# A decoder kernel whose first phase issues each whole-array product as two halves of 64 output partitions

## The reference

```
x = x + L0_attn(layernorm(x))       # mixes x with its shifted copy: dd, then r, k, v, g, w = lerp(...) @ W.T;
                                    # a scan over time for each of 16 heads; group norm; (out * g) @ out_w.T
x = x + L0_xattn(layernorm(x), ctx) # q = x @ wq + b; k, v = ctx @ wk, wv + b, 16 heads of 64, plus 128 memory
                                    # keys and values; softmax(q k / 8) v; @ wo + b
x = x + L0_ffn(layernorm(x))        # router_logits = x @ router_w.T, best 2 of 8 experts
x = x + L1_attn(...); x = x + L1_xattn(...); x = x + L1_ffn(...)
```

## Time and profile before

| | us |
|---|---|
| median of 3 runs | 1446.36 |
| lowest, highest | 1444.64, 1446.71 |
| profiled execution | 1450.02 |
| its span, first to last instruction | 1448.1 |
| TensorE busy in the span | 1312.5 (91%) |
| TensorE weight loads | 964.8 (67%) |
| VectorE busy | 1092.4 (75%) |
| ScalarE busy | 1090.3 (75%) |
| GpSimd busy | 636.4 (44%) |

### The profile page before, as it was taken

How to read it: one execution, slowest core, us unless ns; L and a number is a source line. 1 busy time by engine, 2 the same in 40 slices (tenths; PEclk the granted TensorE clock), 3 DMA queues, 4 the chain that set the end, 5 groups by cost and what they waited for, 6 DMA issues and landing times.

```text
span 1448.1 us, 42973 instructions
## 1 busy us (share of the span) xinstructions
PE 1312.5 (91%) x15457; PEld 964.8 (67%) x15457; DVE 1092.4 (75%) x2601; ACT 1090.3 (75%) x2903; POOL 636.4 (44%) x839
## 2 busy tenths in 40 slices
PE   4259999999999999999984999989989999999996
PEld 1125666666666666667673999967667777777764
DVE  6998889999899988877665344566768788686676
ACT  2128999999999999999992666657677777877763
POOL 0011423353444424320205545357775776655664
PEclk9999999999999999999996999989999999999997
DMA  6942242423224232011013332230101010000000
GB/s 141 245 119 64 52 103 53 101 62 81 60 60 107 56 95 61 16 65 33 24 31 95 91 92 82 58 134 19 31 11 40 10 41 10 24 24 2 25 9 16
DMA packets 82333, 88.49 MB, mean 61 GB/s; under 512 B 15568, under 2 KB 71504, under 8 KB 77520
## 3 DMA queue, kind: packets, MB, share of 16 engines
q1 hardware_dynamic: 77456, 77.10, 20.5%
q0 software_dynamic: 4096, 8.40, 2.0%
q10 hardware_dynamic: 576, 0.26, 0.1%
HBM read 64.76 MB, written 17.83 MB: 57 GB/s over the span
## 4 chain that ended last, share of the span: by engine, by line
PE 64%; DVE 16%; ACT 10%; issue 6%; POOL 2%; DMA 2%; another core or an unknown queue 0%; ACTq 0%; DVEq 0%; SPq 0%; POOLq 0%
PE P L832 7%; PE P L994 7%; PE P L2175 7%; PE P L1615 4%; PE P L1648 4%; PE P L850 3%; PE P L976 3%; ACT pr L1055 3%; PE P L953 3%; PE P L964 3%; PE P L948 3%; PE P L2246 3%; PE P L2193 3%; PE P L2123 2%; PE P L871 2%
## 5 line engine op out<-in xcount | busy, mean ns | idle before, releaser
L1055 ACT ACTIVATE pr<-P,nm 128x256 f32<-128x256 f32 x512 | 239.1, 501 | 6.0 <-DVE nm L1253 5.9
L1253 DVE TENSOR_REDUCE nm<-P 128x4 f32<-128x1024 f32 x128 | 156.2, 1220 | 25.5 <-PE P L832 23.3
L2415 ACT ACTIVATE et<-P 128x1024 f32<-128x1024 f32 x128 | 131.1, 1025 | 42.4 <-PE P L2182 41.4
L832 PE MATMUL P<-kt_w,qt 64*128 64x256 f32 x1024 | 145.2, 402 | 4.6 <-ACT pr L1055 4.6
L1037 ACT COPY ptS<-P 128x512 f32<-128x512 f32 x256 | 138.2, 599 | 8.7 <-PE P L850 8.2
L1028 ACT ACTIVATE pr<-pr,ri 128x256 f32<-128x256 f32 x254 | 119.5, 536 | 24.1 <-DVE pr L1226 23.5
L740 POOL TENSOR_TENSOR kv_qk<-kv_qk,mixing 128x512 f32<-128x512 f32 x48 | 61.1, 1272 | 152.1 <-DVE pr L1226 152.1
L1711 ACT ACTIVATE hT<-P,mixing 128x128 f32<-128x128 f32 x284 | 81.4, 368 | 61.4 <-PE P L1615 54.1
L734 POOL TENSOR_TENSOR kv_qk<-kv_qk,r_w 128x512 f32<-128x512 f32 x48 | 61.0, 1271 | 145.0 <-DVE pr L1226 99.4
L1055 ACT ACTIVATION_READ_ACCUMULATOR pr<-P,nm 128x1 f32 x512 | 118.6, 232 | 0.0
L2553 DVE TENSOR_REDUCE qS<-P 128x8 f32<-128x1024 f32 x64 | 78.3, 1224 | 45.5 <-PE P L2175 45.1
(11 more groups left out here) (373 smaller groups left out, 3828.2 us busy)
## 6 DMA issues: line engine op xcount, KB each, us to landing
kv_qk<-scr_v SPq DMA_DIRECT2D x16, 1024.0 KB, 8.1
r_w<-scr_r SPq DMA_DIRECT2D x16, 1024.0 KB, 10.7
xt<-scr_xs SPq DMA_DIRECT2D x71, 64.0 KB
scr_ys<-yt SPq DMA_DIRECT2D x71, 64.0 KB, 1.5
x<-in_x SPq DMA_DIRECT2D x8, 256.0 KB, 10.2
scr_v<-mixing SPq DMA_DIRECT2D x8, 256.0 KB, 2.5
scr_r<-mixing SPq DMA_DIRECT2D x8, 256.0 KB, 2.0
xb<-in_x SPq DMA_DIRECT2D x8, 256.0 KB, 3.5
```

Of the source, the lines that this page charges most:

```text
L832: m = nc.tensor.matmul(scores(s)[:, hh, cc * KEYS:(cc + 1) * KEYS], QT[part, c, b * T:(b + 1) * T], keys, start=True, stop=True)
L1055: e = nc.scalar.activation(pr[:, s % 3, h * KEYS:(h + 1) * KEYS], scores(s)[:, h // 2, (h % 2) * KEYS:(h % 2 + 1) * KEYS], ACT.Exp, bias=n ...
L1253: nc.vector.tensor_reduce(nm[:, s % 3, 0:4].rearrange("p (a h) -> p a h", a=2), scores(s).rearrange("p a (h k) -> p a h k", k=KEYS), AX.X, ...
L2415: nc.scalar.activation(et[:, u % 4, :, :, :], turned_scores(u), ACT.Exp).then_inc(S["h_exp"], 1)
```

## The change

A helper `product` stands in the first phase's `tensor_program`. It issues one product as two: output partitions 0 to 63 with the weight columns 0 to 63, then 64 to 127 with the columns 64 to 127, both with the same moving operand and the same start and stop flags. The semaphore is raised by the second half. All products of the first phase that used the whole array go through it: dd, r, v, k, w, g, o, out, lg, cum, keys, queries, values, the output projection and the last sums. Not changed are the scores, the weighted sums, and all transposes, those of the whole array among them. No wait and no other engine's program is changed. The second and third phases stay.

```diff
+                def product(out, weights, moving, start=True, stop=True):
+                    for c in range(0, 128, HALF):
+                        m = nc.tensor.matmul(out[c:c + HALF], weights[:, c:c + HALF], moving, start=start, stop=stop)
+                    return m
...
-                        nc.tensor.matmul(bank7, wA[:, 0, :], XS[:, :, 0:T], start=True, stop=True)\
-                          .then_inc(S["b7"], 1)
+                        product(bank7, wA[:, 0, :], XS[:, :, 0:T]).then_inc(S["b7"], 1)
...
-                            m = nc.tensor.matmul(bank7[:, b * T:(b + 1) * T], KV[:, 7, b * T:(b + 1) * T], centre[:, :],
-                                                 start=True, stop=True)
+                            m = product(bank7[:, b * T:(b + 1) * T], KV[:, 7, b * T:(b + 1) * T], centre[:, :])
...
-                            nc.tensor.matmul(P[:, 3, :], wk[:, c * 128:(c + 1) * 128], ctP[:, g % 2, :],
-                                             start=True, stop=True).then_inc(S["b_kp"], 1)
+                            product(P[:, 3, :], wk[:, c * 128:(c + 1) * 128], ctP[:, g % 2, :]).then_inc(S["b_kp"], 1)
...
-                        nc.tensor.matmul(P[:, 4, :], ctP[:, g % 2, b * T:(b + 1) * T],
-                                         wv[:, half * 512:(half + 1) * 512], start=True, stop=True)\
+                        product(P[:, 4, :], ctP[:, g % 2, b * T:(b + 1) * T], wv[:, half * 512:(half + 1) * 512])\
                           .then_inc(S["b_vp"], 1)
...
-                            m = nc.tensor.matmul(P[:, 4, 0:128], aoT[:, b, 4 * half + c, :], wo[:, 4 * half + c, :],
-                                                 start=(c == 0), stop=(c == 3))
+                            m = product(P[:, 4, 0:128], aoT[:, b, 4 * half + c, :], wo[:, 4 * half + c, :],
+                                        start=(c == 0), stop=(c == 3))
```

## The result

The changed kernel takes 1436.01 us (median of 6 runs, 1434.17 to 1436.72) against 1446.53 us for the kernel before (median of 6). The ratio is 0.9928 with a 95% interval from 0.9916 to 0.9940, so 10.5 us less. The forecast was 1433 with a range of 1425 to 1442.

A forecast was written before the change was run, and what follows sets the result against it. TensorE was taken to set the pace, with ScalarE a few per cent behind. Savings of 10.8 + 1.6 + 0.6 + 0.4 = 13.4 us gave 1436.6 from the profiled execution, 1433 us from the median; range 1425 to 1442.

The forecast's parts named there:

- The price of a change of tiling: Packed attention steps: 0.09 us drain and 0.05 and 0.05 us of weight load saved, 5.39 to 5.19 us.
- The two packed steps with whole-array transposes: Steps with L807 or L912: the tiling change only moves, 0.14 us more and 0.14 less, so nothing in sum.
- A pair of halves costs what a whole instruction costs: All split products: halves run side by side, 0.86 us per 512-column product, nothing gained or lost.
- halves in line: Rival: second half starts 0.43 us late at 512 columns, 1447 to 1488 us; chance 0.09 together with any other loss.
- The small bf16 sums: One step of each group: eight whole sums of 0.21 us become sixteen halves of 0.4, 0.2 us more.
- What reaches the end in the middle groups: Nine of sixteen steps keep 0.20 us, 1.8 us a group, 10.8 us for six groups.
- What the transposes wait for: Transposes on TensorE wait 1.1 us in a step where VectorE's normalisation holds ScalarE; steps leading up lose their saving.
- The sign that I had set for the waits: Packed steps at 5.19 us with longer waits between them and a middle group above 83.5 us.
- the waits swallow more: Rival: ScalarE and VectorE hand the saving back as idle time, half lost, 1440 us (1438 to 1443.5); chance 0.20.
- The last two groups: ScalarE is next, idle 0.12 us in a light step; gains of 1.6 us and 0.6 us.
- Before step 0: Half loads save 0.1 us at the lower clock's pace for about four products in the chain: 0.4 us.

The follow-up runs named there:

- the two partial kernels: Against the kernel before: halves only for values, output projection and last sums, 1444.06 us; halves for all products but those, 1454.87 us.
- e_scalar_after: Changed kernel with ScalarE normalising only 64 of each head's 256 probabilities: 1429.40 us, ratio 0.9884 to the kernel before.
- e_both_after: Changed kernel with VectorE's step-7 scan put behind the next normalisation and GpSimd's bias addition held back: 1437.29 us, ratio 0.9946 to the kernel before.
- e_pool_after: Changed kernel with VectorE's running sum moved to GpSimd from the third group on: 1447.22 us, ratio 0.9985 to the kernel before.

## Why the prediction held, point by point

**The price of a change of tiling: right.** 0.20 us for a packed step was forecast, 0.22 measured (5.39 to 5.17), and the two partial kernels show the same price with the other sign: 5.54 with one change more, 5.36 to 5.39 with the same number. The two packed steps with whole-array transposes (3 and 9 of a group) stay at 4.89, as forecast.

**A pair of halves costs what a whole instruction costs: right**, at 128 and at 512 columns. The rival of halves in line is out: it asked for a second half 0.43 us late, and no product shows that. The Trainium skill's rule behind it (TensorE: Matmul & The Clock Gate, Part 3, matmuls start strictly in program order) doesn't describe the two passes of one half and the first pass of the other here: the code issues the whole product of the first half ahead of the second's, and in the trace one matmul of each starts within 10 ns (443.603 and 443.610 us), the next two 0.43 us later, four in 0.86 us in all.

**The small bf16 sums: the term was too large.** 0.2 us more was forecast, 0.06 measured. Within 0.2 to 0.4 us, but at its lower part. The Trainium skill (TensorEngine Tiling (Array Packing), Restrictions: no fast weight load with column tiling) leads one to expect a loss here; the loss is there and small, 0.27 us against 0.21. That it comes from this rule no run here shows.

**The router's logits: a term that I left out.** With 8 columns a product is all weight load. Whole loads follow one another at 0.11 us, pairs of half loads at 0.06: 0.42 us less in step 11. That step saves 0.63 us in six of the eight groups (1 to 6), 0.43 more than another packed step, so 2.6 us in all were in no term of mine. I had read that a pair of halves costs as much as a whole from products of 128 columns, where the streaming takes as long as the load.

**What reaches the end in the middle groups: the term was too large**, and this is the step that made the forecast 3 us too low. I took nine steps at 0.20 us, 10.8 us for six groups; the profiles have 6.1. And 2.1 of these 6.1 are the logits'. In the steps of groups 1 to 4, steps 0, 1, 4 and 13 save 0.2 each, 12 and 15 do in the fifth group alone, and step 11 saves 0.63. But in the last three of these groups step 5 lasts 0.32 to 0.37 us longer than before (5.13 to 5.45 in the fifth) and step 10 0.10 to 0.27; in the second to fourth group step 12 lasts 0.2 longer; steps 7 and 8 stay as they were. I had counted steps that wait for VectorE today as lost, and had not looked at steps that would start to wait. The waits of the fifth group answer to the earlier trace rows:

```profile
PEld P L789 <- ACT ptS L1035: 6.9, 15, 1.3
...
PEld P L856 <- issue: 3.8, 6, 1.4
...
ACT pr L1026 <- DVE pr L1224: 3.3, 4, 1.8
```

For the transposes TensorE's loads wait 3.8 us where it was 2.2, and ScalarE waits for VectorE's normalisation as before, 3.3 us. The first row has the values and the output projection together, since the helper's line is one; before, they were two rows (L976 3.5 us in 7 waits, L964 2.1 in 6), so 6.9 us in 15 waits stand against 5.6 in 13.

What the transposes wait for is not what I had read. I had put their wait down to VectorE's normalisation. But the unit that a step transposes was normalised 5 to 6 us earlier. The code also makes them wait until VectorE has read PSUM bank 4, which they write: the values with their bias (L1205, `V<-P,bv`) or the sum into the residual (L1212, `xb<-xb,P`) of the step before. Steps 5 and 8 of the fifth group, VectorE and TensorE:

```profile
467.41 0.29 DVE L1212 TENSOR_TENSOR xb<-xb,P 128x128 f32<-128x128 f32 x1
467.95 0.71 PE L856 MATMUL P<-ident,pr 64*128 64x64 f32 x16 [0.35 <-DVE xb L1212]
...
482.50 1.21 DVE L1192 TENSOR_TENSOR_SCAN kv_qk<-mixing,kv_qk 128x512 f32<-128x512 f32 x1
483.63 0.66 DVE L1205 TENSOR_TENSOR V<-P,bv 128x512 f32<-128x512 f32 x1
484.50 0.71 PE L856 MATMUL P<-ident,pr 64*128 64x64 f32 x16 [1.02 <-issue]
```

The transposes start 0.25 us after the addition ends in the one and 0.21 in the other, and the same distance, 0.21 to 0.31, stands in every step of this group in which they start late: 2, 5, 8 and 10 before the change; 2, 5, 7, 8, 10 and 14 after it. In step 5 the addition ends 1.22 us into the step, where it was 0.76 before: TensorE's steps 0, 1 and 4 are 0.2 us shorter each, and VectorE, whose instructions follow one another without a gap here, is not faster. That is how savings came to be eaten.

The experiments fit as far as they go: moving work of VectorE or GpSimd shortens the long step and lengthens the next ones, and leaves the sum. That taking VectorE's work away widens the distance is likely but not sure, and an order of VectorE's queue with the bank read ahead of the scan and the norms was not tried on its own.

The sign that I had set for the waits, a group above 83.5 us with packed steps at 5.19, came in two of the four middle groups (83.7 and 83.5). So the rival "the waits swallow more" was right for these groups, where more than half of the forecast 1.8 us was lost; over the whole kernel other terms made up for it.

**The last two groups: right in kind.** ScalarE bounds them, as forecast from the earlier trace rows, and `e_scalar_after` shows it. I took 2.2 us; the profiles say 3 to 5. The logits' step is 0.63 us of the rest. The others I set too low because I took ScalarE's idle time for the bound of each single step: several light steps of the last group but one now take 4.31 us, less than the 4.43 to 4.46 that ScalarE needs in a row of them, and ScalarE catches up in the heavier steps between.

**Before step 0:** 0.4 us was forecast, with a clock at the lower level that I had taken from the pace of one product alone; the windows of the profile list 1.00 for that stretch, so the level is not shown. The profiles show the steps start 2.2 us earlier, the run with halves only there shows no gain above 1.2. Open.

The sum came out near in part by luck: two terms that were too small (the last groups, the logits) stood against one that was too large. Without the 2.6 us of the logits, which I had not seen, the gain would have been some 8 us where 13.4 were forecast.

## What to carry to other kernels

Where products of different array tilings alternate, count the changes in a step: here each cost 0.09 us of drain and 0.05 to 0.105 of uncovered weight load, and giving the products the tiling of their neighbours removes a change at almost no price (0.06 us for the bf16 sums). The halves were issued in turns here; no other order was tried. It only pays if the whole run up to the neighbour is changed; doing a part of it moved the drain or added one. And before taking a saving times the number of steps, look in each step for the engine that is next, since one that shows idle time on the average can have none in the steps that count. Look there for the instruction that empties a PSUM bank: here it stood in VectorE's queue behind a scan, and TensorE waited for it.

## What I had not expected of the hardware

- Products of 8 columns are faster in halves: four fp32 ones took 0.49 us against 0.91, a load for a load: 0.06 us for each pair of halves against 0.11 for a whole.
- A VectorE normalisation of 128 x 256 took 1.40 us instead of 0.35 when a GpSimd instruction followed on another without a hole, and a comparison 1.49 instead of 0.41 when that place moved. Not all VectorE instructions beside GpSimd's are stretched.
- TensorE stopped in the middle of a run of transposes between which no wait stands, in one group of `e_scalar_after`; in another group it stopped inside a first-layer product. The first, in its timeline:

```profile
353.18 0.53 PE L856 MATMUL P<-ident,pr 64*128 64x64 f32 x11
355.94 0.34 PE L856 MATMUL P<-ident,pr 64*128 64x64 f32 x5 [2.23 <-issue]
```

  The idle 2.23 us have no semaphore behind them, and that step took 7.6 us. The profiles have four such stops of over 0.5 us: two here (2.23 us, and 1.24 in the product), one in `e_both_after` (0.69) and one in `e_pool_after` (0.96), none in a kernel with whole products. In each a packet of 16 KB on the queue for instruction code starts 2.6 to 3.0 us before TensorE goes on (353.08 for 355.94) and is there 1.2 to 1.7 us before, while the other transfers fill the DMA engines (the queue q1 alone 99 to 102% of their time). The changed program has 45469 instructions in the record instead of 42973, and the queue for instruction code 139 packets instead of 129. All this points to the code's loading as the cause; it was not tested.
